# Scores and maxima products of an attention kernel, each written as four products of 32 weight columns

## The reference

```python
q, k, v = (split_heads(x @ W) for W in (Wq, Wk, Wv))      # (4, 16, 512, 8)
attn = jnp.einsum('bhqd,bhkd->bhqk', q, k) * e ** (-0.5)
attn = jax.nn.softmax(attn, axis=-1)
attn = attn + bias[None]                                  # bias from rel_table
out = jnp.einsum('bhqk,bhkd->bhqd', attn, v)
```

## Time and profile before

| | |
|---|---|
| median of 3 runs | 329.12 us (329.12 to 329.22) |
| profiled execution, its time | 329.13 us |
| its span | 327.3 us |
| mean granted TensorE clock | 0.996 of 2.4 GHz |
| busy: PE, DVE, ACT, POOL | 297.8, 232.4, 200.8, 126.3 us |

### The profile page before, as it was taken

How to read it: one execution, slowest core, us unless ns; L and a number is a source line. 1 busy time by engine, 2 the same in 40 slices (tenths; PEclk the granted TensorE clock), 3 DMA queues, 4 the chain that set the end, 5 groups by cost and what they waited for, 6 DMA issues and landing times.

```text
span 327.3 us, 4928 instructions
## 1 busy us (share of the span) xinstructions
PE 297.8 (91%) x1634; PEld 123.9 (38%) x1658; DVE 232.4 (71%) x516; ACT 200.8 (61%) x392; POOL 126.3 (39%) x209
## 2 busy tenths in 40 slices
PE   4778979999999989999998999999989999999991
PEld 2544322232222233233553432334542433276481
DVE  4448778788779959877676798776759861156673
ACT  3674366676676656788654677896456779921610
POOL 8492700110105632066255702373368124633133
PEclk9999999999999999999999999999999999999998
DMA  5485593189420202030302040302000100000002
GB/s 163 108 249 155 139 322 92 52 287 300 139 74 4 73 2 76 2 72 4 72 4 72 3 106 3 73 2 74 2 2 0 36 3 1 2 0 2 0 0 64
DMA packets 28246, 23.17 MB, mean 71 GB/s; under 512 B 6542, under 2 KB 26686, under 8 KB 28222
## 3 DMA queue, kind: packets, MB, share of 16 engines
q1 hardware_dynamic: 27950, 22.73, 24.7%
q10 hardware_dynamic: 272, 0.13, 0.1%
HBM read 12.18 MB, written 10.52 MB: 69 GB/s over the span
## 4 chain that ended last, share of the span: by engine, by line
PE 65%; DVE 14%; POOL 6%; ACT 6%; issue 4%; DMA 3%; SPq 1%; POOLq 0%; DVEq 0%
PE sm_ps L1132 16%; PE ov_ps L1161 14%; PE st_ps L1143 10%; DVE neg_max L828 8%; PE mi_ps L1255 6%; PE si_ps L1179 4%; ACT probs L703 3%; PE si_ps L1167 2%; PE st_ps L1384 2%; DVE stats L867 2%; DMA k_stack<-stack_dram 1%; PE si_ps L1185 1%; PE si_ps L1240 1%; PE st_ps L1185 1%; PE si_ps L1260 1%
## 5 line engine op out<-in xcount | busy, mean ns | idle before, releaser
L828 DVE TENSOR_REDUCE neg_max<-sm_ps 128x1 f32<-128x512 f32 x256 | 167.3, 684 | 45.0 <-PE sm_ps L1132 43.4
L703 ACT ACTIVATE probs<-st_ps 128x512 f32<-128x512 f32 x256 | 138.0, 610 | 47.9 <-PE st_ps L1143 35.5
L1132 PE MATMUL sm_ps<-k_stack,q_stack 96*128 96x512 bf16 x256 | 98.0, 384 | 9.3 <-DVE neg_max L828 5.7
L1143 PE MATMUL st_ps<-q_stack,k_stack 128*128 128x512 bf16 x233 | 78.6, 380 | 2.1 <-ACT bias_v L614 0.9
L1161 PE MATMUL ov_ps<-probs,v_cur 128*32 128x512 f32 x512 | 68.7, 605 | 0.0
L1132 PEld LDWEIGHTS sm_ps<-k_stack,q_stack 96*128 96x128 bf16 x256 | 24.6, 96 | 100.0 <-DVE neg_max L828 82.3
L467 POOL TENSOR_TENSOR hid<-hid,w_rows 128x512 f32<-128x512 f32 x26 | 33.1, 1275 | 48.8 <-ACT w_rows L614 48.8
L1143 PEld LDWEIGHTS st_ps<-q_stack,k_stack 128*128 128x128 bf16 x256 | 25.2, 99 | 29.1 <-ACT probs L703 9.3
L1255 PE MATMUL mi_ps<-x_t,down_sb 128*128 128x512 f32 x48 | 25.1, 604 | 0.5 <-ACT shift_rows L614 0.5
L891 DVE SCALAR_TENSOR_TENSOR hid<-tanh_sb,mi_ps 128x512 f32<-128x512 f32 x24 | 16.3, 679 | 12.5 <-ACT tanh_sb L740 12.5
L1179 PEld LDWEIGHTS si_ps<-up_sb,hid 128*128 128x128 f32 x192 | 23.3, 192 | 1.0
(11 more groups left out here) (162 smaller groups left out, 293.6 us busy)
## 6 DMA issues: line engine op xcount, KB each, us to landing
stack_dram<-parts SPq DMA_DIRECT2D x18, 384.0 KB, 4.6
q_stack<-stack_dram SPq DMA_DIRECT2D x16, 288.0 KB
k_stack<-stack_dram SPq DMA_DIRECT2D x16, 288.0 KB
stack_dram<-parts SPq DMA_DIRECT2D x6, 288.0 KB, 4.8
x_sb<-L_attn_x SPq DMA_DIRECT2D x4, 256.0 KB, 3.2
out<-y_out SPq DMA_DIRECT2D x3, 256.0 KB, 2.3
stack_dram<-parts SPq DMA_DIRECT2D x6, 96.0 KB, 2.1
down_sb<-L_ffn_values_down SPq DMA_DIRECT2D x1, 512.0 KB, 8.0
```

Source lines behind the costliest of these rows:

```text
L703: nc.scalar.activation(probs[:, u % 2, j, :], st_ps[:, score_bank(u * J + j), :], ACT.Exp, scale=SCORE_SCALE).then_inc(probs_ready, 1)
L828: nc.vector.tensor_reduce(neg_max[:, g % 2, col:col + 1], sm_ps[:, c % 2, :], AX.X, ALU.max, negate=True).then_inc(max_ready, 1)
L1132: nc.tensor.matmul(sm_ps[:, c % 2, :], q_stack[0:SHIFT_ROW, h, c * P:(c + 1) * P], k_stack[0:SHIFT_ROW, h, :], start=True, stop=True).then ...
L1143: nc.tensor.matmul(st_ps[:, score_bank(k), :], k_stack[:, g * J + j, kc * P:(kc + 1) * P], q_stack[:, g * J + j, :], start=True, stop=True ...
```

## The change

Each maxima product and each scores product is written as four products of 32 weight columns with the same 512 moving columns, each for its own 32 partitions of the bank. The semaphore is raised by the last of the four. Waits, banks, order of the calls, and everything on the other engines stay.

```diff
@@ maximum_scores
-                nc.tensor.matmul(sm_ps[:, c % 2, :], q_stack[0:SHIFT_ROW, h, c * P:(c + 1) * P],
-                                 k_stack[0:SHIFT_ROW, h, :], start=True, stop=True).then_inc(sm_ready, 1)
+                for n in range(P // TILE):
+                    first = c * P + n * TILE
+                    i = nc.tensor.matmul(sm_ps[n * TILE:(n + 1) * TILE, c % 2, :],
+                                         q_stack[0:SHIFT_ROW, h, first:first + TILE],
+                                         k_stack[0:SHIFT_ROW, h, :], start=True, stop=True)
+                i.then_inc(sm_ready, 1)
@@ scores
-                nc.tensor.matmul(st_ps[:, score_bank(k), :],
-                                 k_stack[:, g * J + j, kc * P:(kc + 1) * P],
-                                 q_stack[:, g * J + j, :], start=True, stop=True).then_inc(scores_ready, 1)
+                for m in range(P // TILE):
+                    first = kc * P + m * TILE
+                    i = nc.tensor.matmul(st_ps[m * TILE:(m + 1) * TILE, score_bank(k), :],
+                                         k_stack[:, g * J + j, first:first + TILE],
+                                         q_stack[:, g * J + j, :], start=True, stop=True)
+                i.then_inc(scores_ready, 1)
```

## The result

The changed kernel takes 331.78 us (331.57 to 333.45, 5 runs) against 329.22 us (329.12 to 330.94) measured beside it: 1.0084 times, 95% interval 1.0055 to 1.0114. It is slower, by 2.6 us; 6.0 had been forecast. The profiled execution took 331.57 us with a span of 329.8.

What follows compares the result with a forecast made beforehand. TensorE was taken to bound 18 of 63 intervals between values calls, a VectorE loop others. Terms 5.4 - 2.4 + 1.0 + 1.0 + 0.5 + 0.5 = +6.0 us on 329.13 gave 335.1 us, range 329.3 to 344.

Steps and rivals of the forecast that it cites:

- the changes of width: TensorE drains where weights switch between 32 columns and wider: 0.092 us each, 160 instead of 146, 1.3 us of loss.
- The price of a group: Four 32-column bf16 products start every 0.240 us instead of 0.218: 0.022 us more for each of 512 groups.
- interval bound by TensorE: Between values calls where TensorE alone sets the time: 18 of 63, +0.36 or +0.18 us each, together +5.4.
- 12 intervals with four changes: Those of the 18 TensorE-bound intervals that now hold four width changes: +0.36 us each.
- The loop through VectorE: In 16 intervals without a job, maxima, reduces and values form a loop that loses two changes: -0.15 us each, -2.4.
- The 21 units with slack: Other intervals of 8 groups: 16 with two changes taken as 0, five with four changes +1.0 us together.
- Feeding: Groups of 8 instructions at 0.03 us each arrive late where TensorE's queue is empty, at 5 places: +0.5 us.
- the rival of the starved queue: Few instructions decoded ahead of a semaphore wait; 37 intervals with slack lose about 0.3 each: +11, some 346 us; 15%.
- the sentence on 0.25 us a group: Four matmuls at about 62 ns of sequencer time each would add 0.01 us a group, 4 us at most.
- The early part: Up to 42 us: 5 width changes and 27 groups, 1.05 us of TensorE work, half counted: +0.5 us.
- The rival by which a group costs no more than one product: Group at 0.218 us, shortened loop gains in all units with slack: -2.3, 326.8 us; chance 11%.
- the 16 mixed ones: Intervals with slack and two changes, between -0.15 and +0.18 us each, taken as 0; this rival gave them -2.4.

Runs made afterwards that it cites:

- two half-changes: Against the kernel before: only the maxima products as four of 32 columns, 343.07 us (1.0427 times); only the scores products as four, 351.43 us (1.0686 times).

## Why the prediction was wrong

The direction, and the changes of width as its carrier, held. The size did not: 6.0 us were forecast and 2.6 measured. Groups that start 0.218 apart were the first thing that the prediction named as a sign of being wrong, and they do.

**The step that failed is "The price of a group".** It put 0.022 us more on each group of four. The measured price in a stream is nothing: 0.22 from start to start in both forms. I had read the surcharge from passes 0.45 apart in the trace of before, and all of those stood behind a drain. The bias products were taken as a second witness, but they too are islands between products of 128 columns, so both witnesses had the same flaw. The two half-changes show it, and so do the bias products of the changed kernel (0.25 in place of 0.27). That alone takes 0.18 off every interval bound by TensorE, 3.2 us in 18. The same misreading hid a gain: the values' own passes shrink by 0.05 a call once their neighbours are narrow. The two intervals bound by TensorE that had four `x1t` transposes as their job (two changes before, two after) became 0.05 shorter each where +0.18 was forecast.

**What was missed on the other side** is the late second pass: an f32 product of 128 columns that begins behind a drain starts together with its own first load, and its second pass is 0.10 late. All 17 `down` products that stand behind a 32-column product show 0.533; in steady streams it is 0.43. The `up` products do the same: in all 10 places behind a 32-column product the second pass comes 0.21 after the first, where it is 0.11 in a stream. The prediction had no term for this. The trace of before had a few such passes, behind waits. For the 8 of the 12 intervals with four changes that hold a `down` the parts are now 0.18 (two more changes) - 0.05 (values) + 0.10 (`down`) + some 0.03 to 0.04 (starts behind a drain, about 0.01 each), about 0.27 against the measured 0.28 to 0.29. The other four, with `up`, grew by 0.28 to 0.33 and were not taken apart.

**The changes of width** at 0.092: confirmed by distances of 0.31 to 0.33 in every kernel. Their count, 160 against 146, was right, and so was the reasoning that they would leave the units with slack and appear in the bound ones.

**The loop through VectorE**: -0.15 was forecast for each of 16, and -2.2 in all was measured. The 14 units in round 0 and the start of round 1 gave -2.3, seven of them -0.21 to -0.29, since the loop also holds a values call that got shorter; two late ones that I had counted with them lost 0.07 each and are no such loop.

**The 21 units with slack**: 0 and +1.0 forecast, -0.5 and +0.1 measured, nearer to the lower bounds given, for the same reason.

**Feeding**: +0.5 forecast, none. The starts in the earlier trace rows showed 0.03 an instruction where the queue was empty, and I took it for a rate. The same place in the changed kernel, timelines of the weight loads and of TensorE:

```profile
59.10 0.13 PEld L1134 LDWEIGHTS sm_ps<-k_stack,q_stack 96*32 96x32 bf16 x4 [0.48 <-issue]
59.13 0.40 PE L1134 MATMUL sm_ps<-k_stack,q_stack 96*32 96x512 bf16 x4
59.35 0.40 PE L1149 MATMUL st_ps<-q_stack,k_stack 128*32 128x512 bf16 x4
```

The 0.03 between the first load and the first product is there, but it is paid once: the fourth product starts 0.01 behind the first, and the next group 0.22 behind it. In none of the 512 groups does the fourth start come more than 0.022 us behind the first. With the rate falls the rival of the starved queue, and with it the sentence on 0.25 us a group.

**The early part**: half of 1.05, +0.5. Counted from the first early maxima product, it was +0.5 (25.1 against 24.6), by a loss and a gain that partly cancel.

The rival by which a group costs no more than one product was right about its condition and wrong about its end. It let all units with slack win 0.15, where the 16 mixed ones gave 0.5 in all and not 2.4, and it did not know of the late second pass; the kernel got slower all the same.

## What to carry to other kernels

The width of the weights is a property of the neighbourhood and not of the product: count the changes of width in the order of TensorE's queue, price them at what one row shows (0.09 us here), and ask in which stretches they stand. Convert whole runs of neighbours or nothing: either half alone cost 4 to 7%, both together 0.8%, and both with their jobs gained 1.3%, or 1.7% with the early maxima left wide between wide neighbours. A price read next to a drain, a wait or a restart is not the price in a stream; look for a witness with equal neighbours, and where there is none, keep both values in the sum.

## What the hardware showed that I had not expected

- Four bf16 products of 32 columns and 512 moving columns, side by side, start every 0.22 us as a group, the same as one of 128 columns; in a stream their loads lie under the products ahead of them.
- A group behind a change of width starts 0.31 after the 0.22-us product before it. For f32 of 512 columns the four starts then spread over 0.02 us and the next pass comes at 0.45 in place of 0.43.
- An f32 product of 128 columns that starts with its own load has its second pass 0.10 us late: 0.53 against 0.43 in 17 of 17 `down` behind a change of width, 0.21 against 0.11 in 10 of 10 `up`, and 0.53 behind a wait without a change.
- TensorE took 13 ns an instruction over 128 instructions in a row. Where the queue was empty 30 ns passed from the first load to the first product, and the three other products of the group followed within 10 ns.
